# A graph network with segment maxima on one core: the order of the second merge, and register loads of sixteen words instead of eight

## What is computed

```python
def _egnn_conv(x, src, dst, edge_attr, W_msg, W_edge, W_root, b):
    msg = x[src] @ W_msg + edge_attr @ W_edge
    agg = jax.ops.segment_max(msg, dst, num_segments=x.shape[0])
    agg = jnp.where(jnp.isneginf(agg), 0.0, agg)
    return agg + x @ W_root + b
c1 = leaky_relu(_egnn_conv(X, ..., W1_msg, W1_edge, W1_root, b1))
c2 = leaky_relu(_egnn_conv(c1, ..., W2_msg, W2_edge, W2_root, b2))
out = _layernorm(x + c2, axis=-1)
```

## Time and profile before

| | us |
|---|---|
| median of 3 runs (range) | 2060.19 (2059.29 to 2060.62) |
| the profiled execution's own time | 2056.28 |
| its span in the trace | 2054.5 |
| busy: PE, DVE, POOL, ACT | 1648.0, 1329.4, 1219.3, 1085.5 |
| first merge, about | 552 to 992 |
| second merge, about | 1510 to 2054 |

### The profile page before, as it was taken

How to read it: one execution, slowest core, us unless ns; L and a number is a source line. 1 busy time by engine, 2 the same in 40 slices (tenths; PEclk the granted TensorE clock), 3 DMA queues, 4 the chain that set the end, 5 groups by cost and what they waited for, 6 DMA issues and landing times.

```text
span 2054.5 us, 38144 instructions
## 1 busy us (share of the span) xinstructions
PE 1648.0 (80%) x11634; PEld 1385.5 (67%) x11634; DVE 1329.4 (65%) x2435; ACT 1085.5 (53%) x2452; POOL 1219.3 (59%) x1307
## 2 busy tenths in 40 slices
PE   4899999999876777766699999999987766656553
PEld 2378888888766666666477777778776665556552
DVE  4375555555544444444377777777728999999997
ACT  1144444444223334434366666666627777777776
POOL 7777777777244444444577777777747555545432
PEclk9799999999999999999899999999999988898976
DMA  4377878787545666666477777777758888888885
GB/s 70 73 195 223 235 220 236 218 235 221 183 154 204 212 226 231 238 244 233 155 209 214 207 210 213 209 204 222 205 195 251 255 258 260 263 263 266 261 259 141
DMA packets 537287, 440.17 MB, mean 214 GB/s; under 512 B 444819, under 2 KB 446170, under 8 KB 537098
## 3 DMA queue, kind: packets, MB, share of 16 engines
q1 hardware_dynamic: 469324, 282.86, 47.6%
q0 software_dynamic: 38032, 77.00, 13.8%
q10 hardware_dynamic: 29742, 77.88, 10.1%
HBM read 264.25 MB, written 173.37 MB: 213 GB/s over the span
## 4 chain that ended last, share of the span: by engine, by line
PE 42%; DVE 25%; POOL 18%; issue 12%; DMA 2%; ACT 1%; SPq 1%; DVEq 0%; POOLq 0%; ACTq 0%
POOL arena L359 16%; PE ps L537 15%; PE ps L456 10%; DVE stats L923 6%; PE ps L447 5%; DVE arena L921 5%; PE ps L427 4%; DVE arena L918 4%; DVE onehot L903 4%; PE ps L416 2%; PE ps L421 2%; PE ps L435 2%; DMA arena<-nodes,src_perm 1%; DVE small L934 1%; DVE small L930 1%
## 5 line engine op out<-in xcount | busy, mean ns | idle before, releaser
L537 PE MATMUL ps<-hold,onehot 128*128 x4688 | 651.3, 300 | 309.0 <-POOL onehot L404 154.1
L537 PEld LDWEIGHTS ps<-hold,onehot 128*128 128x128 f32 x4688 | 604.9, 210 | 356.7 <-issue 356.1
L359 POOL DMA_INDIRECT arena<-in_x_dram,src_all x392 | 377.6, 963 | 135.4 <-issue 115.7
L456 PEld LDWEIGHTS ps<-w_root,onehot 97*128 97x128 f32 x3136 | 395.5, 192 | 91.3 <-issue 90.9
L359 POOL DMA_INDIRECT arena<-nodes,src_perm x392 | 370.1, 944 | 126.4 <-issue 123.6
L456 PE MATMUL ps<-w_root,onehot 97*128 97x128 f32 x3136 | 413.6, 275 | 0.0
L843 DVE TENSOR_TENSOR_SCAN arena<-keep,arena,ps 96x512 f32<-96x512 bf16 x196 | 248.5, 1268 | 168.5 <-PE ps L427 167.8
L903 DVE TENSOR_TENSOR onehot<-count,rel 128x1024 f32<-128x1024 bf16 x147 | 188.9, 1285 | 257.2 <-PE ps L537 206.2
L657 ACT COPY arena<-ps 128x384 f32<-128x384 f32 x392 | 166.3, 475 | 314.7 <-PE ps L537 314.7
L404 POOL CAST onehot<-keep 128x1024 f32<-128x1024 uint8 x147 | 197.2, 1342 | 201.1 <-ACT ps L643 160.3
L375 POOL CAST arena<-onehot 128x1024 uint8<-128x1024 f32 x147 | 153.9, 1047 | 256.7 <-DVE onehot L903 256.6
(11 more groups left out here) (105 smaller groups left out, 1578.2 us busy)
## 6 DMA issues: line engine op xcount, KB each, us to landing
root<-arena ACTq DMA_DIRECT2D x196, 384.0 KB
arena<-root SPq DMA_DIRECT2D x196, 384.0 KB, 5.2
nodes<-arena SPq DMA_DIRECT2D x49, 768.0 KB, 4.1
arena<-nodes SPq DMA_DIRECT2D x98, 384.0 KB
arena<-in_x_dram SPq DMA_DIRECT2D x97, 384.0 KB
arena<-in_x_dram SPq DMA_DIRECT2D x48, 768.0 KB, 7.1
out_dram<-arena SPq DMA_DIRECT2D x48, 768.0 KB, 4.9
keep<-onehot_bytes POOLq DMA_DIRECT2D x147, 128.0 KB, 4.1
```

Source lines behind the costliest of these rows:

```text
L359: nc.gpsimd.indirect_dma_start(out=gathered[t.ring][0:t.p, i, 0:D], out_offset=None, in_=table_in, in_offset=bass.IndirectOffsetOnAxis(ap= ...
L456: last = nc.tensor.matmul(no_ps[m % 2][:, i * P:(i + 1) * P], nodes_t[m % NODE_RING][0:D + 1, i * P:(i + 1) * P], w_root[0:D + 1, layer * ...
L537: nc.tensor.matmul(ps[:, bass.ds(place_at, P)], onehot[:, k % NS, i, :], flat[:, bass.ds(chunks[i % WORDS], P)], start=False, stop=True, s ...
```

## The change

Registers: `WORDS` goes from 8 to 16; TensorE loads 16 words of each row before every even batch and none before an odd one, in both merges. The second merge: the leaky ReLU reads its first operand from the PSUM banks and its second from the evacuated copy; the seed of a group waits for that instruction (`vec_2`) and no longer for the evacuation; ScalarE evacuates both halves, then does the square root and the normalising of s-1, then the four seeds; ScalarE normalises 11 blocks and VectorE 5, one instruction each; two additions of statistics become one reduction. The first merge keeps its order.

```diff
-WORDS = 8
+WORDS = 16
-        ACT_BLOCKS = 13
+        ACT_BLOCKS = 11
...
                 for k in range(NBATCH):
                     n = min(BATCH, T - k * BATCH)
-                    chunks, places = load_words(0, k * BATCH, WORDS), load_words(PLACES_ON, k * BATCH, WORDS)
+                    if k % 2 == 0:
+                        words = min(WORDS, TP - k * BATCH)
+                        chunks, places = load_words(0, k * BATCH, words), load_words(PLACES_ON, k * BATCH, words)
+                    at = k % 2 * BATCH
...
-                if n >= RING:
-                    act.wait_ge(evacuated[layer], n - RING + 1)
+                if n >= RING and layer == 0:
+                    act.wait_ge(evacuated[0], n - RING + 1)
+                elif n >= RING:
+                    act.wait_ge(vec_2, X_ADDED * ((n - RING) // SG) + 1)
...
+                    if layer == 0:
+                        for h in (2 * s, 2 * s + 1):
+                            evacuate(h)
+                            reseed(h)
+                        continue
                     evacuate(2 * s)
+                    evacuate(2 * s + 1)
+                    if s:
+                        deviation(s - 1)
+                        normalise(s - 1)
                     reseed(2 * s)
-                    evacuate(2 * s + 1)
-                    if layer == 1 and s:
-                        deviation(s - 1)
                     reseed(2 * s + 1)
-                    if layer == 1 and s:
-                        normalise(s - 1)
...
-                next_step(nc.vector.scalar_tensor_tensor(y, y, SLOPE, y, ALU.mult, ALU.max))
+                sums = slot[:, s % 2 * SG:(s % 2 + 1) * SG, :, 0:D].rearrange("p b j d -> p (b j) d")
+                y_blocks = y.rearrange("p (j d) -> p j d", d=D)
+                next_step(nc.vector.scalar_tensor_tensor(y_blocks, sums, SLOPE, y_blocks, ALU.mult, ALU.max))
...
-                nc.vector.tensor_tensor(mean, even, odd, ALU.add)
-                next_step(nc.vector.tensor_tensor(var, stats[:, :, 2], stats[:, :, 5], ALU.add))
+                next_step(nc.vector.tensor_reduce(both, stats[:].rearrange("p j (h c) -> p j c h", c=3)[:, :, 1:3, :], mybir.AxisListType.X, ALU.add))
...
-                then(nc.vector.tensor_tensor(own, own, inv_b, ALU.mult))
-                nc.vector.tensor_tensor(own, own, shift_b, ALU.add).then_inc(norm_v, 1)
+                for j in range(ACT_BLOCKS, RI):
+                    own = y[:, j * D:(j + 1) * D]
+                    last = nc.vector.tensor_scalar(own, own, inv[:, j:j + 1], shift[:, j:j + 1], ALU.mult, ALU.add)
+                last.then_inc(norm_v, 1)
```

More of the change, by code:

```diff
@@ L107, in gnn @@
         stats = sb("stats", [P, RI, 6], F32)
-        small = sb("small", [P, 8, RI], F32)
+        small = sb("small", [P, 9, RI], F32)
         eps = sb("eps", [P, 1], F32)
@@ L121, in gnn @@
         x_in = [arena[:, UNIT_RING * UW + (3 + i) * SW:UNIT_RING * UW + (4 + i) * SW] for i in range(2)]
-        assert BATCH == 2 * C and NODE_RING == 2 * NS and EDGE_RING == 4
+        assert WORDS == 2 * BATCH and BATCH == 2 * C and NODE_RING == 2 * NS and EDGE_RING == 4
         BW = BATCH * P
@@ L533, in merge @@
                     for i in range(n):
[L534 to L537, removed]
+                        place_at = within(places[at + i], (RING * C - 1) * P)
+                        nc.tensor.matmul(ps[:, bass.ds(place_at, P)], onehot[:, k % NS, i, :], flat[:, bass.ds(chunks[at + i], P)],
                                          start=False, stop=True, skip_group_check=True).then_inc(stepped[layer], 1)
@@ L924, in finish @@
                 next_step(last)
-                mean, diff, var = (small[:, i, :] for i in range(3))
+                both = small[:, 0:2, :].rearrange("p c j -> p (c j)").rearrange("p (j c) -> p j c", c=2)
+                mean, spread, diff, var = both[:, :, 0], both[:, :, 1], small[:, 8, :], small[:, 2, :]
                 dev, inv, shift = (small[:, i, :] for i in (3, 4 + 2 * (s % 2), 5 + 2 * (s % 2)))
@@ L930, in finish @@
                 nc.vector.tensor_tensor(diff, even, odd, ALU.subtract)
-                nc.vector.tensor_tensor(mean, even, odd, ALU.add)
-                next_step(nc.vector.tensor_tensor(var, stats[:, :, 2], stats[:, :, 5], ALU.add))
+                next_step(nc.vector.tensor_reduce(both, stats[:].rearrange("p j (h c) -> p j c h", c=3)[:, :, 1:3, :], mybir.AxisListType.X, ALU.add))
                 then(nc.vector.scalar_tensor_tensor(diff, diff, 0.25, diff, ALU.mult, ALU.mult))
-                nc.vector.scalar_tensor_tensor(var, var, 1.0 / D, diff, ALU.mult, ALU.add).then_inc(var_done, 1)
+                nc.vector.scalar_tensor_tensor(var, spread, 1.0 / D, diff, ALU.mult, ALU.add).then_inc(var_done, 1)
                 dve.wait_ge(dev_done, s + 1)
@@ L938, in finish @@
                 dve.wait_ge(norm_set, s + 1)
-                left = RI - ACT_BLOCKS
-                own = y.rearrange("p (j d) -> p j d", d=D)[:, ACT_BLOCKS:, :]
-                inv_b, shift_b = (a[:, ACT_BLOCKS:].rearrange("p (j a) -> p j a", a=1).broadcast_to([P, left, D]) for a in (inv, shift))
-                then(nc.vector.tensor_tensor(own, own, inv_b, ALU.mult))
-                nc.vector.tensor_tensor(own, own, shift_b, ALU.add).then_inc(norm_v, 1)
+                for j in range(ACT_BLOCKS, RI):
+                    own = y[:, j * D:(j + 1) * D]
+                    last = nc.vector.tensor_scalar(own, own, inv[:, j:j + 1], shift[:, j:j + 1], ALU.mult, ALU.add)
+                last.then_inc(norm_v, 1)
             keep_row()
```

## The result

The changed kernel takes 2093.9 us (median of 4 runs, 2092.74 to 2105.53), the kernel before 2059.74 beside it; the ratio is 1.0182, 95% interval 1.0154 to 1.021. The forecast was 2041. The outcome is that of rival C (2088).

The account below looks back on a forecast made before the run. It took TensorE's sequencer to bound the first merge and VectorE the second. Execution 2056.3 - 45 (first merge) + 26 (second merge) = 2037, with 3.9 for the median of runs 2041 us; range 1985 to 2080.

Parts of the forecast that it names:

- rival C: Whole kernel slower, 2088 us: sixteen-word loads cost 1.18 us, first merge gives 2, second loses 28 to 34; chance 0.17.
- part 1: First merge, TensorE's register loads: sixteen words cost 0.99 us plus delays, 53 us gained, 45 kept.
- Part 3: Second merge: seeds behind normalising close a loop over ScalarE, GpSimd and TensorE; period 11.1 instead of 10.5, +29 us.
- The loop's fixed part: Second merge: normalising, seeds, cast, evacuation and square root sum to 8.26 us, without the pair's remaining steps.
- early ends: Second merge: pairs with few steps left before evacuation, where VectorE's own 9.8 to 10.2 us holds instead of 11.4.
- Part 2: Second merge, VectorE's work: slope stays 1.75 us, chain falls from 10.5 to 9.8 us a super-block at best.
- the mutual waiting: Second merge: VectorE's slope and GpSimd's cast shut each other out; a PSUM operand ends it, up to 0.3 us a super-block.
- B: First merge: sixteen-word loads cost hardly more than eight, 75 us gained; second still loses; total 2011 us, chance 0.15.
- A: Second merge gets faster too, 10.0 us a super-block, 24 us gained; total 1989 us, chance 0.20.
- D: First merge: other waits, such as VectorE's one-hot product, fill the gap; gain only 20 us, total 2066, chance 0.10.

Follow-up runs that it names:

- order alone: Kernel before with only ScalarE's order of the second merge changed, slope from SBUF, eight words: 2155.3 us, ratio 1.047.
- gate: Changed kernel with GpSimd waiting for seeds at each batch, only for that batch's groups, instead of each pair: 2040.3 us, ratio 0.990.
- place of the seeds: Changed kernel with the four seeds after 7 of the 11 normalised blocks instead of after all: 2083.3 us, ratio 1.0096.
- the old order stands: Changed kernel with ScalarE's order, slope operand, seeds' wait and loads taken back; new blocks and statistics kept: 2066.0 us, ratio 1.0028.

## Why the prediction was wrong, point by point

**The step that failed is part 1, the price of a load of sixteen words.** I took 0.99 us and 0.42 of delay, 1.41 together; the mean in the first merge was 1.61. The cause was the choice of 0.2 us an access from ScalarE's two-word load, where the doubling from 8 words (the upper bound, 1.18) was nearly right, and the "middle" for the delays, which go by words; the middle of 0.59 and 1.18 is also 0.89 and not the 0.84 used, which is worth 3 us. That takes 73.5 x 2 x (1.61 - 1.41) = 29 us of the 53 that the sum had before the 8 taken off. Of the other 24, 5 were gained, and most of the rest went into a wait for which the sum had only those 8: with the loads in one lump, the second batch of a pair comes 1.1 us behind the first, and its one-hot matrices are at times not made. In the trace after, the gaps of more than 0.06 us over the usual ahead of the register operations that wait for a batch add up to 18 us, before to 1.6; 17 of the 24 such gaps after, with 16.7 us, end 0.04 us behind the end of one of VectorE's one-hot products. The kernel before with sixteen words shows the same: 17 gaps, 13.2 us. No run takes this wait away, so its price is read and not tested.

**Part 3 was right in mechanism and too small in size.** Period 11.1 forecast, 11.38 measured; 26 us forecast, 41 measured. The loop's fixed part holds to 0.2 us in the turn shown: 8.26 forecast, 8.1 measured if the step's end to evacuation is left at 0.25. Why the size was off is open. Too many early ends were not assumed: 15 of the 48 periods are under 10.3 us, with a mean of 9.5, and the other 33 have a mean of 12.2. VectorE's own blocks cost 1.2 us instead of 0.8, but ScalarE's square root waited for VectorE in 15 turns only, so that this explains 15 x 0.4 = 6 us at most, an estimate. The runs support the loop from four sides: order alone +94, gate -50, place of the seeds -12, and no such loss where the old order stands (550.0, +6).

**Part 2:** the slope's price and the end of the mutual waiting came as written (addition of x 1.76 in all 49), though the waiting ended mostly by the new order, as told above, and it gave nothing, since VectorE was no longer the bound; its busy time fell by 37 us. The own blocks start 0.24 us apart where nothing delays them: 1.2 us, inside the bounds of 0.55 to 1.35 and above the value taken. One reading was loose: in the earlier trace rows the clock over the second merge is 0.8 to 0.9 in all slices but the last two, which have 0.7 and 0.6.

**The rivals.** C happened, nearly to its number: the first merge gave 5 us instead of 2, the second cost 41 instead of 30. B is out: the price of a load grows nearly in proportion. A's faster second merge came only when the gate was narrowed. D is part of the truth: a wait for one-hot matrices, as it names one, took 16.7 us. The point at which I let C decide, a load with its delay above 1.6 us, was met at 1.61. The slower outcome had been given a chance of 0.21, and the range ended at 2080, below its middle.

## What to carry to other kernels

When a producer is moved behind a long piece of work on its engine, look for what that engine does next: if the next instruction waits for what the producer releases, a loop is closed, and its length is the sum of the links however much slack each engine shows. A gate over several units makes such loops; narrowing it to one batch gave back 50 us here, where the old order in its place gave 35 (with loads of eight words). That a stage gets shorter by the price of the work taken off an engine does not show that this engine is the bound; see who waits for it. And a register load of four words or more is work on TensorE's sequencer whose price goes nearly by words, so fewer and longer loads save little.

## What the runs showed of the hardware

- TensorE's register loads take 0.33, 0.59 and 1.10 us for 4, 8 and 16 words, at the least; in the first merge sixteen words took up to 3.8 us. With the stores of finished super-blocks the mean for eight words was 0.89 us there, without them 0.67.
- A cast on GpSimd that began inside VectorE's slope took 2.02 us on average where the slope read two operands from SBUF (32 casts), and 1.04 where one operand lay in PSUM (21 casts in seven runs).
- Two broadcast instructions on 288 columns cost 0.92 us undelayed; five `tensor_scalar` on 96 columns with scalars from SBUF start 0.24 us apart undelayed, 1.2 us in all.
- The clock granted to TensorE in the second merge was 0.87 before, 0.80 in the changed kernel and 0.76 with the order alone; with the narrow gate on the kernel before it was 0.91. In the turn at 1761.36 us sixteen steps behind 3.98 us of idle time took 6.42 us at 0.57; eight steps at full speed take 2.05. A pause is thus paid for twice in such a loop.
